# The last chunk's attention in stretches of 256, 128 and 128 queries instead of two of 256

## What is computed

```python
# attention, x: [16, 2048, 1024], causal
Q, K, V = split_heads(x @ WQ.T), split_heads(x @ WK.T), split_heads(x @ WV.T)
e    = exp(scores - max)            # scores = Q K^T / 8, -1e9 above the diagonal
out  = (e / sum(e)) @ V
x    = layernorm(x + merge(out) @ WO.T)
# feed-forward with quantized activations
xn   = x * rsqrt(mean(x*x) + 1e-6)
xq   = round(xn * s) / s            # s = 127 / max|xn| of the row
x    = layernorm(x + xq @ (w_int8 * weight_scale).T + bias)
```

## Time and profile before

| | us |
|---|---|
| median of 3 runs | 1007.29 (1006.96 to 1008.47) |
| the profiled execution | 1006.75 |
| its span on the slowest core (core 1) | 1004.6 |
| spans of the other cores | 999.1 to 1003.6 |
| TensorE busy, of the span | 901.4 (90%) |
| ScalarE busy | 677.8 (67%) |
| VectorE busy | 524.4 (52%) |

### The profile page before, as it was taken

How to read it: one execution, slowest core, us unless ns; L and a number is a source line. 1 busy time by engine, 2 the same in 40 slices (tenths; PEclk the granted TensorE clock), 3 DMA queues, 4 the chain that set the end, 5 groups by cost and what they waited for, 6 DMA issues and landing times.

```text
span 1004.6 us, 22672 instructions; the slowest of 8 cores (999.1 to 1004.6 us)
## 1 busy us (share of the span) xinstructions
PE 901.4 (90%) x8416; PEld 416.6 (41%) x8416; DVE 524.4 (52%) x1269; ACT 677.8 (67%) x707; POOL 226.8 (23%) x289
## 2 busy tenths in 40 slices
PE   3895999999999999899999999999899998888863
PEld 1342444444444444444444444444344444444431
DVE  0110147834875337752148727862577523676665
ACT  0133756777787788888834666777677778989931
POOL 5022422322222111211122322232122111121201
PEclk9997999999999999999999999999999999999987
DMA  9999141530132122241071331141313210123222
GB/s 125 149 177 205 32 54 33 106 106 12 34 85 80 49 33 48 59 106 48 7 96 38 95 117 23 47 133 54 49 33 106 80 33 9 31 65 100 59 58 63
DMA packets 99289, 71.18 MB, mean 71 GB/s; under 512 B 70384, under 2 KB 88816, under 8 KB 99184
## 3 DMA queue, kind: packets, MB, share of 16 engines
q1 hardware_dynamic: 78368, 50.87, 19.7%
q0 software_dynamic: 20816, 18.88, 14.2%
HBM read 55.05 MB, written 16.78 MB: 71 GB/s over the span
## 4 chain that ended last, share of the span: by engine, by line
PE 68%; DMA 9%; ACT 7%; DVE 6%; issue 6%; DVEq 2%; POOL 1%; POOLq 0%; ACTq 0%; SPq 0%
PE ps L322 43%; PE ps L628 13%; PE ps L529 13%; ACT PT L557 6%; DMA WV<-wvt 4%; DMA QO<-OS 3%; DVE OS L664 2%; DMA XT<-xt 1%; ACT Q L826 1%; DVE SM L760 1%; DVE Z L890 1%; DMA QT<-QB 1%; DVEq L663 1%; DVE SM L757 1%; DVE SM L763 1%
## 5 line engine op out<-in xcount | busy, mean ns | idle before, releaser
L557 ACT ACTIVATE PT<-ps,SM 128x1024 bf16<-128x1024 f32 (+2 forms) x576 | 580.6, 1066 | 179.2 <-PE ps L529 176.2
L572 POOL TENSOR_TENSOR PT<-PT,MASK 128x256 bf16<-128x256 bf16 (+1 forms) x184 | 158.2, 867 | 540.0 <-ACT PT L557 539.9
L628 PEld LDWEIGHTS ps<-VX,PT 128*128 128x128 bf16 x4352 | 186.9, 98 | 185.0 <-issue 125.0
L628 PE MATMUL ps<-VX,PT 128*128 128x65 bf16 x4352 | 231.5, 194 | 29.2 <-DVE OS L664 28.5
L529 PE MATMUL ps<-QO,KT 64*128 64x512 bf16 (+1 forms) x1504 | 186.1, 324 | 23.7 <-ACT PT L557 20.6
L322 PE MATMUL ps<-XT,WK 128*128 128x512 bf16 x512 | 131.6, 383 | 19.2 <-DMA XT<-xt 18.9
L322 PE MATMUL ps<-W,QT 128*128 128x512 bf16 x512 | 135.2, 382 | 14.8 <-DMA QT<-QB 14.5
L322 PE MATMUL ps<-WO,QO 128*128 128x512 bf16 x512 | 134.8, 378 | 3.7 <-issue 2.2
L322 PE MATMUL ps<-WV,XT 128*128 128x512 bf16 x512 | 129.6, 385 | 3.9 <-DMA WV<-wvt 3.3
L322 PE MATMUL ps<-XT,WQ 128*128 128x512 bf16 x512 | 131.5, 378 | 0.6 <-DMA WQ<-wqt 0.6
L529 PEld LDWEIGHTS ps<-QO,KT 64*128 64x128 bf16 x1504 | 53.9, 94 | 174.2 <-issue 167.9
(11 more groups left out here) (50 smaller groups left out, 549.1 us busy)
## 6 DMA issues: line engine op xcount, KB each, us to landing
Z<-x SPq DMA_DIRECT2D x32, 512.0 KB, 4.1
y<-Z SPq DMA_DIRECT2D x32, 512.0 KB, 3.1
XT<-xt POOLq DMA_DIRECT2D x7, 1024.0 KB, 11.9
WK<-wkt POOLq DMA_DIRECT2D x4, 512.0 KB, 20.4
WQ<-wqt POOLq DMA_DIRECT2D x4, 512.0 KB, 23.3
WV<-wvt POOLq DMA_DIRECT2D x2, 1024.0 KB, 41.2
WO<-wot POOLq DMA_DIRECT2D x1, 2048.0 KB, 68.2
W<-w8t POOLq DMA_DIRECT2D x1, 2048.0 KB, 83.3
```

Source lines behind the costliest of these rows:

```text
L557: emit("s", lambda eng: eng.activation(dst, src, AF.Exp, bias=EB, scale=0.125).then_inc(sem["s"], 1))
L572: emit("g", lambda eng: eng.tensor_tensor(blk, blk, msk, ALU.mult).then_inc(sem["m"], 1))
L628: last = eng.matmul(ps[:, 2048 + s_ * 512 + q * 65: 2048 + s_ * 512 + q * 65 + 65], PT[:, pt0 + s_ * 512 + c0: pt0 + s_ * 512 + c0 + 128], ...
```

## The change

Of the last chunk, queries 256 to 511 (tiles 30 and 31) are no longer one stretch but two of 128 queries. A stretch with one tile gets units of four blocks of 128 keys: unit kind `"f"` has the diagonal block and the two or three blocks before a multiple of four, the others four whole blocks. Eight head pairs of tile 30 take 4 units each (the first of 3 blocks), eight of tile 31 take 4 each (of 4 blocks), so there are again 64 units. `wo` of tile 30 now waits for the stretch of tile 30 alone. Its blocks are put on the list at the start of the chunk, `behind([30])`, and only tile 31's come after the last P·V. The number of gaps over which the list is spread is lowered by 8.

```diff
-        subs += [(NCH - 1, 0, 2), (NCH - 1, 2, 2)]
+        subs += [(NCH - 1, 0, 2), (NCH - 1, 2, 1), (NCH - 1, 3, 1)]
...
-                else:
+                elif nq == 2:
                     kinds = ["e"] + list(range(0, first_k, 2))
+                else:
+                    kinds = ["f"] + list(range(first_k % 4, first_k, 4))
...
+            if nq == 1:
+                keys = ([k0] + list(range(k0 % 4)) if kd == "f"
+                        else list(range(kd, kd + 4)))
+                return [(k, j * 128, q0 * 128, 128)
+                        for j, k in enumerate(keys)]
...
+            if nq == 1:
+                if kd == "f":
+                    return ([(k, 0, 128 + k * 128) for k in range(k0 % 4)],
+                            [(k0, 0, 0)])
+                return [(kd + j, 0, j * 128) for j in range(4)], []
...
-            su = g if g < NCH - 1 else g + r // 2
+            su = g if g < NCH - 1 else g + max(0, r - 1)
...
             if g == NCH - 1:
-                mine += behind([4 * g, 4 * g + 1])
+                mine += behind([4 * g, 4 * g + 1]) + behind([4 * g + 2])
...
-            todo = 2 * len(pairs[g])
-            gaps = [todo]
+
+            gaps = [2 * len(pairs[g]) - (8 if g == NCH - 1 else 0)]
...
-        main.extend(behind([4 * NCH - 2, 4 * NCH - 1]))
+        main.extend(behind([4 * NCH - 1]))
```

More of the change, by code:

```diff
@@ L481, in build_nc @@
                     kinds = ["d0", "d1", "d2"] + list(range(first_k))
+                elif nq == 2:
+                    kinds = ["e"] + list(range(0, first_k, 2))
                 else:
-                    kinds = ["e"] + list(range(0, first_k, 2))
+                    kinds = ["f"] + list(range(first_k % 4, first_k, 4))
                 for kd in kinds:
@@ L549, in emit_s @@
             s0 = (u % 2) * 1024
-            if kd in ("d2", "e"):
-                c0, nc_ = (256, 256) if kd == "d2" else (0, 384)
+            if kd in ("d2", "e", "f"):
+                c0, nc_ = {"d2": (256, 256), "e": (0, 384),
+                           "f": (0, 128 * len(mm))}[kd]
                 dst = ap(PT, pt0 + c0, (4096, 128), (512, 2), (1, nc_))
@@ L563, in emit_s @@
                           + 60.0 + 1.97 * cols)
-            if kd in ("d0", "d1", "d2", "e"):
+            if kd in ("d0", "d1", "d2", "e", "f"):
                 wait("g", tok_exp[u], tok_consts2[0])
                 m0, step_, nb = {"d0": (0, 128, 1), "d1": (0, 128, 2),
-                                 "d2": (256, 128, 1), "e": (0, 256, 2)}[kd]
+                                 "d2": (256, 128, 1), "e": (0, 256, 2),
+                                 "f": (0, 128, 1)}[kd]
                 blk = ap(PT, pt0 + m0, (4096, 128), (512, 2), (step_, nb),
```

## The result

The changed kernel took 1018.5 us (median of 4 runs, 1016.18 to 1061.01) against 1007.88 (4 runs, 1006.96 to 1092.1): **slower, ratio 1.0097, 95% interval 1.0074 to 1.0121**. In a few executions one die ran at a lower clock (the 1061.01 and the 1092.1 are such); the ratios leave them out. 1009.0 was forecast, with a range to 1014. The direction was right, the size was not.

The account below looks back on a forecast made before the run. ScalarE and TensorE, both near their limits, were taken to bound the attention, and a chain with no engine full the tail. Attention +5.7 and tail −3.9 gave +1.8: 1008.6 profiled, 1009.0 us median, range 1003 to 1014.

Parts of the forecast that it names:

- First stretch, +1.5 forecast: Attention's first stretch: 25 pairs at 2.34, three empty pairs and three `quant` take 68.2 us against 66.7, +1.5.
- Second half, +4.2 forecast: Attention's second half: pairs 75.3, `quant` 1.9, hand-overs 0.8 and clock 2.2 sum to 80.2 us against 76.0, +4.2.
- The term for sixteen hand-overs, +0.8: Second half: eight more hand-overs between head pairs, each with a division on VectorE, cost +0.8 us (0 to 3).
- The term for the clock, +2.2: Second half: three more long filler-free runs let TensorE fall to half speed, +2.2 us (0 to 6).
- +1.2 for the moved blocks: Second half: pairs priced by their fillers sum to 75.3 us against 76.0 before, plus 1.9 for `quant`.
- Tail, −3.9 forecast: From the last exponential's end: one tile less in the chain shortens it by 3.9 us (−5.6 to −2.2).
- that block's price: Tail: `ffn` 30 starts 5.1 us after the last exponential and ends at 8.6.
- C: Rival, clearly slower: filler-free runs drop TensorE to 1.2 GHz and the next fillers start at half speed; attention +10, 1013; chance 0.20.
- D: Rival: S matmuls of 128 columns cost far more than their columns, 81 ns each; +15, 1024 us; chance 0.03.
- The transposes on SyncE's queue: Attention: 8 more transposes of 1.2 us on SyncE cause no wait, 2 us if a load blocks the queue.

Follow-up runs that it names:

- split alone: The changed kernel, but with tile 30 finished after the last P·V and the gap budgets of the kernel before; ratio to the kernel before 1.0027.

## Why the prediction was wrong

**First stretch, +1.5 forecast, +7.5 measured: the step that failed.** The sum had 25 pairs at 2.34, three empty ones and a third `quant`, 68.2 us. With the rule that keeps the hand-overs short it takes 68.8. What failed is that the term counts only what ScalarE and TensorE have to do. It left the hand-overs at their price before, "the division (two instructions) on VectorE, with a queue of statistics before it", and looked for a change of that queue only in the second half, at +0.8. The bigger budgets move every due step of the planner against the units. P·V waits rose by 5.3 us and ScalarE's idle time by 6.6. Of the 7.5 us, 5.4 go with the rule; the other 2.1 stand against the forecast's 1.5 for the third `quant` and the fillers, which was nearly right.

**Second half, +4.2 forecast, +3.0 measured.** The pairs came nearly as priced. Six fillers give 2.5: two pairs from 921.95 to 926.94 in ScalarE's timeline. A pair without filler takes 2.0: five in 10.15 us, the last row.

```profile
921.95 2.12 ACT L565 ACTIVATE PT<-ps,SM 128x1024 bf16<-128x1024 f32 x2 [0.75 <-PE ps L536]
924.28 1.91 ACT L565 ACTIVATE PT<-ps,SM 128x768 bf16<-128x768 f32 x2 [0.21 <-PE ps L536]
926.94 2.12 ACT L565 ACTIVATE PT<-ps,SM 128x1024 bf16<-128x1024 f32 x2 [0.76 <-PE ps L536]
...
963.54 10.15 ACT L565 ACTIVATE PT<-ps,SM 128x1024 bf16<-128x1024 f32 x10 [1.90 <-PE ps L536]
```

The term for sixteen hand-overs, +0.8, had the wrong sign, as split alone shows: P·V waits there were 1.5 us against 2.6. The term for the clock, +2.2, rests on three filler-free runs at half clock. Only the run around the border was, from within or shortly behind the wait of 3.1 us on; the two others, near 950 and 968 us on core 0, ran at full clock at 2.0 us a pair, but for 3.4 us in the last one on core 2. Filling the gaps won nothing in either case. A third term was too small and hides both: by its pairs and `quant` (75.3 + 1.9 against 76.0) the sum had +1.2 for the moved blocks. Split alone has 104 fillers before its last exponential and 74.2 us, the changed kernel 119 and 78.8, so +4.6 on top of a split that takes 1.6 off. That the total of this part came within 1.2 us is in part luck.

**Tail, −3.9 forecast, −2.4 measured** (41.8 against 42.8 on the slowest cores). TensorE and `quant`, core 0:

```profile
973.51 1.30 ACT L840 ACTIVATE Q<-Z,SM 128x1024 f16<-128x1024 f32 x1
...
978.89 5.30 PE L322 MATMUL ps<-W,QT 128*128 128x512 bf16 x16 [2.11 <-DMA QT<-QB]
...
984.18 3.61 PE L322 MATMUL ps<-WO,QO 128*128 128x512 bf16 x16
...
995.92 1.24 ACT L840 ACTIVATE Q<-Z,SM 128x1024 f16<-128x1024 f32 x1 [5.61 <-DVE SM L827]
997.27 0.43 DVE L847 TENSOR_SCALAR QB<-Q 128x1024 bf16<-128x1024 f16 x1 [1.49 <-ACT Q L840]
...
1001.03 6.30 PE L322 MATMUL ps<-W,QT 128*128 128x512 bf16 x16 [13.24 <-DMA QT<-QB]
```

`ffn` 30 starts 5.2 us after the last exponential (5.1 forecast), `wo` 31 stands behind it, and `integers` of tile 31 waits for `quant` alone, all as the prediction had it. But `ffn` 30 took 5.30 and not 3.5, with TensorE in part at half clock there too: +1.8. The term that failed here is that block's price. And `ffn` 31 took 6.30 where 5.30 was the sum's value: +1.0. Together they are 2.8 of the 2.9 us between −3.9 and the slowest core's −1.0. On core 5, where `ffn` 30 ran in 3.61 and `ffn` 31 in 5.05, the tail was 39.1, near the forecast's 38.9.

**The rivals.** C had the right sign and, with 1013, came nearest (the profiled execution took 1017.0), but for another reason: clock and hand-overs at 0.4 us. The hand-overs cost up to 3.1, in a stretch where C had none. D is out. Sixteen S matmuls of 128 columns took 0.62 us at full clock, eight 0.40, so 0.03 us each:

```profile
963.04 0.62 PE L536 MATMUL ps<-QO,KT 64*128 64x128 bf16 x16
...
964.80 0.40 PE L536 MATMUL ps<-QO,KT 64*128 64x128 bf16 x8 [0.52 <-ACT PT L565]
```

The Trainium skill gives about 81 ns a matmul at this width ("TensorE: Matmul & The Clock Gate", section "Back-to-back issue gap"), by estimate 1.3 us for sixteen; the trace does not agree (0.62 us), and the measurement decides, as the prediction took it. The transposes on SyncE's queue blocked nothing: on core 0 no division in this chunk waited for one.

## What to carry to other kernels

Where a planner interleaves several chains, a change of its budgets moves every due step. Before the pairs' contents are priced, find the short instruction that hands a buffer from one group of work to the next, and read from the new order what stands ahead of it on its engine, and what that waits for. Be wary of a step ahead of such a hand-over whose input comes from a third engine: a rule in the planner, "nothing from the queue between the last P·V and the division", held the hand-over at 0.6 to 1.0 us in the three kernels that had it. The same rule moved `quant` by one or two exponentials, which was worth 1.2 us in one of them, so look at every engine's order after such a rule. Judge a lowered clock by where it stands: in the attention, which other waits bound, filling it up won nothing, and in the tail, a chain, `ffn` 31 took 6.30 us where at full clock it took 3.61.

## What was unexpected

The same 112 fillers in the first stretch gave 68.8, 71.3 and 74.2 us, in the same pairs, by the order on VectorE and GpSimd, engines that are busy 38.9 and 11.3 of 74.7 us. In other pairs they gave 70.8. Two extra matmuls in every empty gap raised the granted clock of the second half from 0.93 to 1.00 and didn't shorten it. Filler-free runs of four and five pairs kept the full clock, but for one core in one of them, and the run that followed a wait of 3.1 us didn't. And after some 52 extra matmuls and 3 us of idle time the next block began at half clock on six of eight cores, and on two it didn't.
